# Second convolution's aggregate: the fourth head's weights multiplied in on GpSimd, the other three on VectorE

## What is computed

```python
def gatv2_conv(x, src, dst, Wl, Wr, att, bias):
    xl = (x @ Wl).reshape(n, H, D)              # H = 4 heads, D = 128
    xr = (x @ Wr).reshape(n, H, D)
    m = jax.nn.leaky_relu(xl[src] + xr[dst], NEG_SLOPE)
    e = jnp.einsum('ehd,hd->eh', m, att)
    ...
    alpha = ex / (denom[dst] + 1e-16)           # softmax over the edges of a target, per head
    out = jax.ops.segment_sum(alpha[:, :, None] * xl[src], dst, num_segments=n)
    return out.mean(axis=1) + bias
...
h = jax.nn.relu(layer_norm(gatv2_conv(h0, ...1), g1, be1) + h0)
h2 = layer_norm(gatv2_conv(h, ...2), g2, be2)
return h2 + h
```

## Time and profile before

| | us |
|---|---|
| median of 3 runs | 4792.28 |
| lowest, highest | 4786.27, 4793.47 |
| the profiled execution, its time | 4799.01 |
| the profiled execution, span from first to last instruction | 4797.0 |
| second aggregate, first to last multiplication of `weigh` | 3186.3 to 3517 |

### The profile page before, as it was taken

The page is one execution under the profiler, slowest core; times in us unless marked ns, Lnnn a source line. Parts: engine busy times, 40 slices in busy tenths (PEclk is TensorE's granted clock), DMA queues, the critical chain, the costliest instruction groups (busy, mean ns, idle before and its releaser), DMA issues. The chain is left out here.

```text
span 4797.0 us, 66181 instructions
## 1 busy us (share of the span) xinstructions
PE 3393.7 (71%) x14380; PEld 1894.6 (39%) x14380; DVE 3285.1 (68%) x10437; ACT 2668.4 (56%) x7608; POOL 2889.3 (60%) x2835
## 2 busy tenths in 40 slices
PE   1544188544998979997797999948855649974332
PEld 1534133222665633432564344325532215543331
DVE  1322199775996768887786888869978868874332
ACT  1422299796776757775575777726657735530000
POOL 4777687687984457773687555315567600027776
PEclk9656599655999989998898999979978869985555
DMA  8433288796668966664896444459979956753331
GB/s 290 124 97 92 102 282 278 290 406 252 201 190 269 307 194 209 212 212 143 273 323 217 154 158 157 135 195 338 337 239 342 336 164 216 229 185 105 98 99 53
DMA packets 685509, 1019.82 MB, mean 213 GB/s; under 512 B 109779, under 2 KB 293748, under 8 KB 683248
## 3 DMA queue, kind: packets, MB, share of 16 engines
q1 hardware_dynamic: 617296, 877.29, 55.0%
q0 software_dynamic: 65856, 113.13, 9.0%
q10 hardware_dynamic: 2016, 25.69, 1.3%
HBM read 640.44 MB, written 381.14 MB: 213 GB/s over the span
## 5 line engine op out<-in xcount | busy, mean ns | idle before, releaser
L984 DVE TENSOR_TENSOR conv_logits_leaky<-conv_logits_z,conv_logits_sloped 128x512 f32<-128x512 f32 x784 | 516.9, 687 | 117.8 <-ACT conv_logits_sloped L918 102.0
L918 ACT ACTIVATE conv_logits_sloped<-conv_logits_z 128x512 f32<-128x512 f32 x784 | 459.1, 596 | 175.9 <-PE conv_logits_z L880 123.5
L1250 PE MATMUL conv_aggregate_part<-conv_aggregate_weighed,conv_wlc 128*128 128x512 f32 x784 | 360.0, 602 | 39.8 <-DVE conv_aggregate_weighed L1332 39.8
L880 PE MATMUL conv_logits_z<-conv_logits_hdT,conv_logits_wsum 128*128 128x512 f32 x784 | 368.0, 613 | 4.7 <-DVE conv_logits_leaky L984 2.7
L887 PE MATMUL conv_logits_z<-conv_diffT,conv_logits_wl 128*128 128x512 f32 x784 | 352.9, 593 | 0.0
L1570 ACT ACTIVATE conv_nodes_squares<-conv_nodes_o_ps 128x128 f32<-128x128 f32 x784 | 206.5, 278 | 165.7 <-PE conv_nodes_o_ps L1492 165.7
L1332 DVE TENSOR_TENSOR conv_aggregate_weighed<-conv_aggregate_alpha,conv_diffT 128x512 f32<-128x512 f32 x392 | 259.8, 722 | 9.5 <-DMA conv_aggregate_alpha<-ALPHA 9.5
L117 POOL DMA_INDIRECT AGG<-gine_edges_rows,idx x196 | 194.0, 990 | 103.1 <-issue 101.9
L1492 PEld LDWEIGHTS conv_nodes_o_ps<-conv_nodes_wmean,conv_nodes_hT 128*128 128x128 f32 x1568 | 191.3, 192 | 160.3 <-DVE conv_nodes_hT L1528 81.4
L1959 PE MATMUL mean_edges_turned<-mean_edges_ident,mean_edges_hs 128*128 128x128 f32 x196 | 54.6, 434 | 277.7 <-DMA mean_edges_hs<-H,idx 277.7
L111 POOL DMA_INDIRECT gat_logits_hs<-H,idx x196 | 214.4, 1094 | 59.8 <-issue 56.8
(11 more groups left out here) (294 smaller groups left out, 10205.0 us busy)
## 6 DMA issues: line engine op xcount, KB each, us to landing
conv_aggregate_alpha<-ALPHA SPq DMA_DIRECT2D x392, 256.0 KB, 5.3
HX<-gine_finish_hx SPq DMA_DIRECT2D x98, 512.0 KB, 11.7
AGG<-gine_edges_zero ACTq DMA_DIRECT2D x14, 1792.0 KB, 34.2
gine_mlp_x<-x SPq DMA_DIRECT2D x98, 256.0 KB
gine_mlp_agg<-AGG SPq DMA_DIRECT2D x98, 256.0 KB
YT<-gine_mlp_yT SPq DMA_DIRECT2D x98, 256.0 KB, 4.2
gine_finish_x<-x SPq DMA_DIRECT2D x98, 256.0 KB, 7.1
gine_finish_yT<-YT SPq DMA_DIRECT2D x98, 256.0 KB, 11.5
```

The lines of the kernel that those rows point to most:

```text
L880: pe.matmul(z[h][:, :], wsum[:, h * D:(h + 1) * D], hdT[j % 3][:, :], start=True, stop=True).then_inc(z_done[0], 1)
L918: act.activation(sloped[(H * (2 * j + c) + h) % S][:, :], z[h][:, :], ACT.Copy, scale=SLOPE).then_inc(sloped_made[c], 1)
L984: dve.tensor_tensor(leaky[H * c + h][:, :], z[h][:, :], sloped[(H * (2 * j + c) + h) % S][:, :], ALU.max).then_inc(leaky_made[c], 1)
L1250: last = pe.matmul(part[n % 2][:, :], g.wlc[:, h * D:(h + 1) * D], weighed[n % 2][:, h, :], start=(h == 0), stop=(h == H - 1))
```

## The change

In the second convolution's aggregate VectorE multiplies only heads 0 to 2 (`V = 3`), and GpSimd multiplies head 3 in a new step `weigh_last(n)`, first in its turn. The new semaphore `last_weighed` counts it. TensorE waits for it before its fourth head, and SP before it loads over that `alpha` buffer. In the first convolution V stays 4.

```diff
@@ conv_aggregate
     N, final = g.NTE, layer == 1
+    V = H - 1 if final else H
...
+        last_weighed = m.sem("last_weighed")
...
                 def load(n):
-                    past(sp, weighed_made, H * (n - 2))
+                    past(sp, weighed_made, V * (n - 2))
+                    if final:
+                        past(sp, last_weighed, n - 2)
...
                 def await_weighed(n):
-                    wait_alone(pool, weighed_made, H * (n + 1), own)
+                    wait_alone(pool, weighed_made, V * (n + 1), own)
+
+                def weigh_last(n):
+                    wait_alone(pool, alpha_in[n % 3], 64 * (n // 3 + 1), own)
+                    past(pool, part_done, n - 1)
+                    pool.tensor_tensor(weighed[n % 2][:, V, :], alpha[n % 3][:, V, :], g.diffT[:, n * TILE:(n + 1) * TILE], ALU.mult).then_inc(last_weighed, 1)
...
-                sweep(N, [(0, await_weighed), (4, add_base), (0, make_base), (5, add_row) if final else (0, look_up)])
+                sweep(N, ([(0, weigh_last)] if final else []) + [(0, await_weighed), (4, add_base), (0, make_base), (5, add_row) if final else (0, look_up)])
...
                     for h in range(H):
-                        pe.wait_ge(weighed_made, H * n + h + 1)
+                        if h < V:
+                            pe.wait_ge(weighed_made, V * n + h + 1)
+                        else:
+                            pe.wait_ge(last_weighed, n + 1)
...
-                    for h in range(H):
+                    for h in range(V):
                         dve.tensor_tensor(weighed[n % 2][:, h, :], alpha[n % 3][:, h, :], g.diffT[:, n * TILE:(n + 1) * TILE], ALU.mult).then_inc(weighed_made, 1)
```

## The result

The changed kernel takes 4815.4 us (median of 12 runs, 4810.3 to 4822.9) against 4792.8 us of the kernel before, measured beside it (12 runs). The ratio is 1.0045, with a 95% interval of 1.0037 to 1.0054, which is 18 to 26 us more. The profiled execution of the changed kernel has a span of 4810.9 us; the phases ahead of this one happen to be 3.5 us shorter in it than in the first trace and those behind it 3.0 us, so the two spans alone show less of the loss than the phase does.

What follows compares the result with a forecast made beforehand. VectorE's work, transfers and VectorE's waits lay close; the circle through the store bound. Its 7.2 and 7.4 gave 7.3 us a tile: 41 x (7.30 - 7.01) = +11.9 us, 4792.3 + 12 = 4804 us, range 4786 to 4820.

Steps and rivals of the forecast that it cites:

- circle through the store: Two-turn loop from scan via store landing, `x_out` and `res` to VectorE's next scan; binds, rising from 7.01 to 7.2-7.4 us.
- the transfers as a floor: DMA in the middle stretch: true floor between 6.3 and 7.01 us a turn, not binding but capping a gain.
- VectorE's 0.62 us less, GpSimd's 1.23 more: Per tile, VectorE's own turn falls from 6.63 to 6.01 us; GpSimd's added multiplication is priced like its additions, 1.23 us.
- circle on the shared resource: GpSimd's operations and VectorE's multiplications exclude each other; their sum per turn rises from 6.27 to 6.88 us, a new floor.
- case of no difference: Rival: GpSimd's idle time swallows the 1.23 us as stores land sooner (5.2 to 4.6); turn stays 7.01, 4792 us; chance 0.28.
- half a collision: VectorE's multiplications against GpSimd's `base`: 0.15 us more per two turns, as collisions come nearly always when `res` is late.
- slower by more: Rival: early or mid-weighing landings let GpSimd run two operations ahead of VectorE's three; 7.5 to 7.6 a tile, 4816 us; chance 0.15.
- my forecast's own case: Middle stretch of 41 tiles: 7.2 to 7.4 us a tile, +8 to +16 us; chance 0.50.
- Filling and draining: Pipeline's start and end: filling could cost up to 3.7 us over six tiles, or nothing; nothing taken for either.
- SP's added wait costs nothing: SP's wait before loading over `alpha`: free, since the scan it awaits anyway needs the same multiplication.
- TensorE's cover for its fourth head: TensorE's wait for GpSimd's product: covered by 35.6 us free in the stretch, and its output is scanned a turn later.
- The faster case: Rival: landings under 4 us let VectorE's gain through, down to a transfers' floor of 6.65; gain 15 us, 4777; chance 0.07.

Runs made afterwards that it cites:

- e5: The kernel before, unchanged, run on a second chip; 7.07 us a turn, one execution of 5186 us.
- e12: Kernel before, two `x_out` buffers kept, only ScalarE's squares moved into `sumB`'s spent buffer; 7.00 us a turn, ratio 1.0000 to the kernel before.
- e8: Kernel before with three `x_out` buffers instead of two, squares moved to make room; 6.77 us a turn, ratio 0.9973 to the kernel before.
- e9: Changed kernel with three `x_out` buffers, GpSimd's product replaced by two zero fills that read no SBUF; 6.22 us a turn, 0.9946 against the kernel before.
- e10: Changed kernel with three `x_out` buffers, GpSimd's product moved behind its wait for VectorE's other three; 7.19 us a turn, 1.0025 against the kernel before.
- e7: Changed kernel with three `x_out` buffers instead of two, squares moved to make room; 7.24 us a turn, ratio 1.0025 to the kernel before.
- e4: Changed kernel with GpSimd's product moved behind `res`, ahead of `base`; 7.87 us a turn, ratio 1.0067 to the kernel before.
- e1: Fourth head's product left out altogether: VectorE makes three, GpSimd none, against the kernel before; 6.88 us a turn, ratio 0.9984.

## Why the prediction was right or wrong

**The number.** The loss is 22.6 us where I forecast 12: the direction and the mechanism came true, the size came out at that of a rival with a chance of 0.15 (4816 us; measured 4815.4), which had also stretched the range up to 4820. That the range holds the result is owed to this rival and not to the forecast's own 4804. Of the 10.6 us that are missing, 6.9 lie in the stretch of 41 tiles and 1.7 in filling and draining; the other 2 are within the scatter of the runs.

**What bounds.** Right. Three things near each other, of which the circle through the store of `x_out` makes VectorE wait: with a third buffer the wait is gone, and the turn falls from 7.07 (e5; 7.00 in e12) to 6.77, near the 6.63 that I read as VectorE's own work (e8). Wrong was to leave the transfers as a floor that might lie up to 7.01: they carry 383 GB/s at 6.22 us a turn (e9).

**VectorE's 0.62 us less, GpSimd's 1.23 more.** Right as prices. VectorE: 6.77 to 6.22 between e8 and e9, 0.55 us. GpSimd's product alone takes 1267 ns (e10).

**The circle on the shared resource, 6.88 us.** The mechanism was right, the size wrong. Without the store's circle the changed kernel needs 7.19 to 7.24 us (e10, e7). My sum took VectorE's part from the gap between `base` and `x_out` in the trace of before, where POOL waits for a store. In the changed kernel POOL's row starts behind a wait for VectorE's last product, some 0.3 us after it (e10). I had not counted that hand-over, and its 0.27 us are nearly all of 7.2 - 6.88.

**The circle through the store, 7.2 to 7.4 us.** Its direction was right, and two of its terms were off, in opposite directions. Landings fell from a median of 5.2 to 4.7 us, which the case of no difference had said. The term that was mis-sized is the collisions: I added half a collision of 0.29 us for two turns, 0.07 a turn, and measured 0.40 a turn more (0.52 against 0.12). The sooner landings fall into the weighing (in those 11 turns `x_out` starts 1.1 to 1.4 us after the first product, in the trace of before never in less than 2.1), so what the circle gains by them it loses in collisions. That was my "slower by more" (7.5 to 7.6 a turn), to which I had given 0.15; the first trace lies at its edge with 7.47, the second chip's 7.36 in my forecast's own case. The sum of +11.9 us for the stretch was 18.8 in the first trace and 12 on chip 2.

**Filling and draining.** I took nothing and was 1.7 us short.

**SP's added wait costs nothing.** Wrong as told: SP waits 15.4 us for POOL's product and 38.0 for the turned `hd`, 0 and 1.2 before. In the changed kernel that delays little: the issue of the store stays within 1 us behind the scan in 35 of 41 turns (median 0.87, as before), and VectorE never waits for `alpha`. One step further, with the product behind `res`, the store is issued 1.2 us later (e4), and there the waits may be a cause of the loss. TensorE's cover for its fourth head was thin too: for POOL's product its weight loads wait 70.0 us and its matmuls 38.6 in the stretch. VectorE's scan still waits for TensorE in no turn, so such a delay could only come in by way of SP's loads and store. How much of the changed kernel's 0.46 us it makes, no run separates.

**The rivals.** The faster case is refuted as a case of this kernel: dropping the product altogether yields 0.16% (e1), and what would let more through, sooner releases of `x_out`, ends in the exclusion (e7). Where neither the store nor the exclusion stands in the way the turn is 6.22 us (e9), near VectorE's own 6.01 and below the 6.65 that I had taken for the transfers. The case of no difference had its mechanism, sooner landings, but not its outcome.

## What to carry to other kernels

Before work is moved to a half idle engine, ask what its idle time lies ahead of: here 106.5 of POOL's 132.5 idle us were a wait for one store, and an operation behind that store lengthened the row on which the busy engine waits. If both engines can't run such operations at one time, add up their rows over one turn as if they were one engine, with each hand-over between them, and compare that with the turn. Here that sum is 1.9 us of VectorE's products, 5.3 of POOL's four operations and 0.3 of hand-over, 7.5 us against the measured 7.2, since the operations overlap a little at their ends: it is an upper estimate. And where a wait for a buffer shows in the trace, a further buffer is the change to try first: it gave 0.2 to 0.3 us a turn under the kernel before (0.1 under the changed one), while the moved work cost 0.3 to 0.5.

## What the runs showed of the hardware

- VectorE's products with two SBUF inputs and GpSimd's operations that read SBUF alternate: a GpSimd operation can also step in between two products that follow each other without a wait (the changed kernel at 3291.41, 3.25 us for three products instead of 1.88). In the trace of before it came only at the last product. My forecast did not count with it, only its last rival did.
- GpSimd's fills, which read nothing from SBUF, run beside these products: 1.11 us of fills within products of 1.98 us (e9). A fill of 128x512 takes 0.53 us on GpSimd, a product or sum of two such tiles 1.27.
- Nine transfers of 256 KB a turn went through at 383 GB/s with a share of 1.06 (e9), where the same mix had 332 and 0.98 before. So a share of 0.98 was not yet the limit here.
